# Edge messages of a graph layer: the last three groups are left out of the table until its squares have been summed, and the barrier between the two stages goes

## What is computed

```python
h = jnp.maximum(_layernorm(x, axis=-1), 0.0)
z = jnp.concatenate([h[src], h[dst], edge_attr_32], axis=-1)
m = jax.nn.sigmoid(z @ W_f + b_f) * jax.nn.softplus(z @ W_s + b_s)      # one row for each edge
message = jax.ops.segment_sum(m, src, num_segments=100000)
mean = jnp.mean(message, axis=0)
var = jnp.mean((message - mean) ** 2, axis=0)
out = x + h + (message - mean) * jax.lax.rsqrt(var + 1e-5) * gamma + beta
```

## Time and profile before

| | us |
|---|---|
| median of 3 runs | 1090.13 (1090.04 to 1090.58) |
| profiled execution | 1098.08 |
| its span, first to last instruction | 1096.2 |
| POOL busy in the span | 691.6 (63%) |
| DVE busy | 730.7 (67%) |
| ACT busy / PE busy | 541.5 (49%) / 561.5 (51%) |
| first block load of the scan issued | 900.60 |
| last block of the scan landed | 964.70 |

### The profile page before, as it was taken

How to read it: one execution, slowest core, us unless ns; L and a number is a source line. 1 busy time by engine, 2 the same in 40 slices (tenths; PEclk the granted TensorE clock), 3 DMA queues, 4 the chain that set the end, 5 groups by cost and what they waited for, 6 DMA issues and landing times. The chain is left out here.

```text
span 1096.2 us, 10749 instructions
## 1 busy us (share of the span) xinstructions
PE 561.5 (51%) x2286; PEld 386.8 (35%) x2286; DVE 730.7 (67%) x1514; ACT 541.5 (49%) x1201; POOL 691.6 (63%) x606
## 2 busy tenths in 40 slices
PE   1131745566554476374575455765545636744423
PEld 0120533445442354252353234553333425630000
DVE  3211765758766667666686756767657676789978
ACT  1122655456555566464565454755554634644432
POOL 7774777777777787877877778777777540010000
PEclk9985676566576756656766765655666658975555
DMA  8992435345434354334344333334243339979999
GB/s 288 407 388 52 95 82 124 80 115 123 102 93 107 88 121 124 78 61 83 54 85 84 58 82 74 62 87 85 53 85 57 54 59 397 420 273 420 427 427 396
DMA packets 85856, 174.00 MB, mean 159 GB/s; under 512 B 40591, under 2 KB 47411, under 8 KB 77491
## 3 DMA queue, kind: packets, MB, share of 16 engines
q1 hardware_dynamic: 34523, 109.88, 28.4%
q0 software_dynamic: 40768, 19.31, 15.4%
q10 hardware_dynamic: 10520, 44.39, 10.1%
HBM read 105.67 MB, written 67.85 MB: 158 GB/s over the span
## 5 line engine op out<-in xcount | busy, mean ns | idle before, releaser
L411 POOL DMA_INDIRECT xg<-in_x_dram,ids x392 | 375.6, 958 | 120.9 <-issue 116.1
L424 POOL DMA_INDIRECT msgs_dram<-comb,target x196 | 309.6, 1580 | 87.7 <-issue 71.2
L843 PE MATMUL bank_c<-msg,same 128*128 128x64 f32 x980 | 165.8, 343 | 32.8 <-issue 19.7
L843 PEld LDWEIGHTS bank_c<-msg,same 128*128 128x128 f32 x980 | 158.0, 254 | 46.4 <-issue 25.2
L516 DVE TENSOR_REDUCE row_ssq<-sq 128x24 f32<-128x1536 f32 (+2 forms) x53 | 86.5, 1631 | 113.5 <-ACT sq L699 58.9
L811 PE MATMUL bank_c<-ident,eas 128*128 128x128 f32 x49 | 21.2, 432 | 248.8 <-ACT comb L754 247.9
L754 ACT ACTIVATE comb<-bank_c 128x256 f32<-128x256 f32 x49 | 18.6, 380 | 212.0 <-remote 208.2
L832 PEld LDWEIGHTS ps_v<-w_z,z_t 128*128 128x128 f32 x392 | 93.2, 326 | 49.8 <-issue 49.8
L747 ACT ACTIVATE same<-same,one_col 128x512 f32<-128x512 f32 x196 | 107.6, 550 | 1.6
L599 DVE TENSOR_TENSOR msg<-gate,soft 128x256 f32<-128x256 f32 x49 | 20.7, 423 | 126.7 <-issue 71.8
L811 PEld LDWEIGHTS bank_c<-ident,eas 128*128 128x128 f32 x49 | 8.8, 180 | 262.9 <-issue 262.8
(11 more groups left out here) (120 smaller groups left out, 989.0 us busy)
## 6 DMA issues: line engine op xcount, KB each, us to landing
m_buf<-msgs_dram SPq DMA_DIRECT2D x37, 1024.0 KB, 20.6
xn<-in_x_dram SPq DMA_DIRECT2D x48, 512.0 KB
out_dram<-m_buf ACTq DMA_DIRECT2D x20, 1024.0 KB, 10.5
msgs_dram<-y_kept SPq DMA_DIRECT2D x11, 1536.0 KB
src_all<-src_rows_dram SPq DMA_DIRECT2D x46, 256.0 KB
y_spill_dram<-y_kept ACTq DMA_DIRECT2D x19, 512.0 KB
y_kept<-y_spill_dram SPq DMA_DIRECT2D x8, 1024.0 KB, 20.6
msgs_dram<-y_kept ACTq DMA_DIRECT2D x5, 1536.0 KB
```

The source lines that it names most:

```text
L411: pool.indirect_dma_start(xg[:, n % G_SLOTS, 2 * j + c, :], None, x, bass.IndirectOffsetOnAxis(ap=ids[:, c, n * TILES + j:n * TILES + j + ...
L424: pool.indirect_dma_start(msgs, bass.IndirectOffsetOnAxis(ap=target[:, n % UNROLL, j:j + 1], axis=0), comb[:, n % UNROLL, j, :], None, com ...
L843: pe.matmul(ps_c[:, j, :], same[:, b, j, :], msg[:, b, :], start=(b == 0), stop=(b == j))
```

## The change

Stages one and two become one program per engine without a barrier; stage one's buffers now lie in `m_buf`, `m_last` and `sums`, so that the first five blocks of the ring (`FREE_FIRST`) and the others come free at different points. The nodes no longer trail (`SKEW` 0). The messages of groups 46 to 48 (`LATE` = 3) stay on chip (`late_comb`, `late_msg`). POOL gathers the table's rows for their 12 tiles (`was_read`), scatters them into a second table `msgs_late`, gathers them back from there (`added_late`), and DVE works out by how much the squares grow, `late_msg * (2 * was_read + added_late)`, and sums it into `corr_row` (`correct`, after block 15's squares). When the scan's loads have landed, the 12 tiles are added to `msgs` (`add_late`), and after the held blocks are stored, scaled and added to `out` (`patch`). `msgs_late` is filled with zeros, one piece of 512 KB in each step from group 6 on and the rest at group 48. The ring has 8 blocks in place of 9, the edge-attribute ring 3 slots in place of 6, `comb` 3 in place of 6.

```diff
-SKEW = 4
+SKEW = 0
...
-E_SLOTS = 6
+E_SLOTS = 3
+COMB_SLOTS = 3
+LATE = 3
+EARLY = GROUPS - LATE
...
-M_BUFS = 9
+M_BUFS = 8
+FREE_FIRST = 5
...
-Y_AHEAD = 3
+Y_AHEAD = 6
+CORRECT_AT = 15
+LIST_AT = 10
...
+            if not g.known:
+                sp.dma_start(late_rows[:, bass.ds((g.n - UNROLL) * BULK, BULK), :].rearrange("p r f -> p (r f)"),
+                             zeros[:, :]).then_inc(late_zeroed, 16)
...
-            for n in range(behind, GROUPS):
+        for n in range(behind, EARLY):
                 accumulate(n)
-            pool.wait_ge(accumulated, 16 * ALL_TILES)
+        pool.wait_ge(late_listed, 1)
+        pool.wait_ge(ssq_done, STEPS)
+        pool.wait_ge(accumulated, 16 * TILES * EARLY)
+        for k in range(LATE):
+            n = EARLY + k
+            for t in range(k * TILES, (k + 1) * TILES):
+                pool.indirect_dma_start(
+                    was_read[:, t, :], None, msgs, bass.IndirectOffsetOnAxis(ap=late_ids[:, t:t + 1], axis=0),
+                ).then_inc(late_read, 16)
+            pool.wait_ge(comb_copied, n + 1)
+            pool.wait_ge(target_done, n + 1)
+            if k:
+                pool.wait_ge(late_put, 16 * TILES * k)
+            else:
+                pool.wait_ge(late_zeroed, 16 * (LAST - UNROLL + 3))
+            for j in range(TILES):
+                pool.indirect_dma_start(
+                    msgs_late, bass.IndirectOffsetOnAxis(ap=target[:, n % UNROLL, j:j + 1], axis=0),
+                    late_comb[:, k * TILES + j, :], None, compute_op=ALU.add,
+                ).then_inc(late_put, 16)
+        pool.wait_ge(late_put, 16 * LATE_TILES)
+        for t in range(LATE_TILES):
+            pool.indirect_dma_start(
+                added_late[:, t, :], None, msgs_late, bass.IndirectOffsetOnAxis(ap=late_ids[:, t:t + 1], axis=0),
+            ).then_inc(late_got, 16)
...
-            act.wait_ge(spilled, 16 * SPILL)
...
+    def sync(sp):
+        sp.wait_ge(accumulated, 16 * TILES * EARLY)
+        sp.wait_ge(y_done, STEPS)
+        sp.wait_ge(z_turned, GROUPS)
+        sp.wait_ge(ea_turned, GROUPS)
...
+            if b == FREE_FIRST:
+                sp.wait_ge(sum_kept, 1)
+                sp.wait_ge(comb_copied, GROUPS)
+                sp.dma_start(m_rest[:, :], msgs[P * N_ROWS:NODES, :]).then_inc(rest_loaded, 16)
+            if b == NB - 1:
+                sp.wait_ge(corr_done, 1)
...
+        sp.wait_ge(late_added, 16 * LATE_TILES)
+        sp.wait_ge(block_crossed, M_BUFS + 2)
...
+                if k == len(y_parts) - 1:
+                    act.wait_ge(patched, 16 * LATE_TILES)
...
+        def correct():
+
+            dve.wait_ge(late_read, 16 * LATE_TILES)
+            dve.wait_ge(late_got, 16 * LATE_TILES)
+            dve.scalar_tensor_tensor(out=was_read, in0=was_read, scalar=2.0, in1=added_late,
+                                     op0=ALU.mult, op1=ALU.add).then_inc(corr_steps, 1)
...
+            if i == len(held) - 1 and y_parts[k + 1][0] > i:
+                dve.wait_ge(late_added, 16 * LATE_TILES)
...
```

More of the change, by code:

```diff
@@ L60 @@
 assert 0 < LAST_ROWS < BULK
-assert (SPILL + 1 + SKEW) % UNROLL == 0
+assert (SPILL + 1 + SKEW) // UNROLL >= 1 and UNROLL % COMB_SLOTS == 0 and LATE <= UNROLL
 S_BLK = 32
@@ L116, in first_row, with late @@
     @property
+    def late(self):
+        return self.known and self.n >= EARLY
+    @property
     def first_row(self):
@@ L158, in keep @@
             return outer.enter_context(nc.sbuf_tensor(name, shape, dt))
[L160 to L168, removed]
@@ new lines, in build @@
+        at = Shared()
+        at.y_kept = keep("y_kept", [P, KEPT_ROWS, F])
+        at.ones = keep("ones", [P, P])
+        at.ident = keep("ident", [P, P])
+        at.eps_col = keep("eps_col", [P, 1])
+        at.one_col = keep("one_col", [P, 1])
+        at.msg_sum = keep("msg_sum", [P, F])
+        at.small = keep("small", [P, 4])
+        at.target = keep("target", [P, UNROLL, TILES], I32)
+        at.late_comb = keep("late_comb", [P, LATE_TILES, F])
+        at.late_msg = keep("late_msg", [P, LATE_TILES, F])
@@ L377, in _ @@
-            for u in range(SLOTS):
-                load(Group(0, u))
-            sp.wait_ge(zeros_set, 1)
-            done = ZERO_EARLY
-            for u in range(SLOTS, UNROLL + 1):
-                end = min(ZERO_PARTS, 2 * ZERO_EARLY + 1 + 3 * (u - SLOTS))
-                for k in range(done, end):
-                    zero_table(k)
-                done = end
-                if u < UNROLL:
-                    load(Group(0, u))
-            with sp.Fori(1, ITERS) as it:
-                for u in range(UNROLL):
-                    load(Group(it, u))
@@ L391, in _ @@
-            for u in range(GROUPS - LAST + SKEW):
-                load(Group(ITERS, u))
+            one.sync(sp)
+            two.sync(sp)
         @block.gpsimd
         def _(pool):
-            pool.sem_inc(slots_free, UNROLL - 1)
-            pool.memset(ident[:, :], 0.0).then_inc(masks_set, 1)
-            pool.memset(upto[:, :], 1.0).then_inc(masks_set, 1)
-            pool.wait_ge(masks_set, 2)
-            pool.affine_select(out=ident[:, :], in_=ident[:, :], compare_op=ALU.not_equal, fill=1.0,
-                               base=0, pattern=[[-1, P]], channel_multiplier=1).then_inc(masks_made, 1)
@@ L444, in _ @@
[L444 to L446 removed]
+            one.gpsimd(pool)
+            two.gpsimd(pool)
         @block.vector
         def _(dve):
[L450 to L455 removed]
@@ L649, in _ @@
-            for u in range(1, UNROLL):
-                step(Group(0, u), True)
-            first_kept = (SPILL + 1 + SKEW) // UNROLL
-            with dve.Fori(1, first_kept) as it:
-                for u in range(UNROLL):
-                    step(Group(it, u), True)
-            with dve.Fori(first_kept, ITERS) as it:
-                for u in range(UNROLL):
-                    step(Group(it, u), False)
-            for u in range(STEPS - LAST + 1):
-                step(Group(ITERS, u), False)
@@ L780, in _ @@
-            for u in range(UNROLL):
-                step(Group(0, u), True)
-            first_kept = (SPILL + 1 + SKEW) // UNROLL
-            with act.Fori(1, first_kept) as it:
-                for u in range(UNROLL):
-                    step(Group(it, u), True)
-            with act.Fori(first_kept, ITERS) as it:
-                for u in range(UNROLL):
-                    step(Group(it, u), False)
-            for u in range(STEPS - LAST + 1):
-                step(Group(ITERS, u), False)
```

1980 lines of the change are left out of this document (1103 added, 877 removed).

## The result

The changed kernel takes 1099.46 us (median of four runs, 1098.57 to 1101.91), the kernel before 1090.32 beside it (1090.04 to 1090.58). The ratio is 1.009, with a 95% interval of 1.0078 to 1.0103: the change costs 9 us. The prediction had 1083.6 and a faster kernel at 0.62, a slower one at 0.28. The time lies inside its range, on the wrong side. The profiled execution took 1099.36, with a span of 1097.6.

What follows compares the result with a forecast made beforehand. POOL's indirect DMAs were taken to bound stage one, the DMA engines the scan and output part. -17.5 (scan) + 7 (output part) + 4 (start) = -6.5 from 1090.1 gave 1083.6 us, range 1070 to 1102.

Steps and rivals of the forecast that it cites:

- Steps 1 and 2: End of stage one: five early scan loads leave at 864.5, 36.1 us earlier; the sixth load's wait opens at 888.
- Steps 2 and 3: Scan from 888: ramp 3.3, remaining blocks 49.6, POOL's 36 indirect DMAs 6.3 us; last block lands 947.2, 17.5 us gained.
- Step 4: Scan: POOL's correction data arrive at 921 to 928, DVE finishes at 939 to 946, just before the last block; cost 0.
- The rule of the Trainium skill: Scan: DMA engines take turns between queues packet by packet, so landings stay in the single figures of us.
- Step 5: Output part, after the scan's last block lands: one more block reloaded, late reloads and patches together cost +7 us.
- The ring's 2.5: Output part: the ring holds 8 blocks, so one more is reloaded, 1.05 MB at 427 GB/s, +2.5 us.
- their lateness: Output part: reloads wait for the late scatters, until 38 us after the scan's last block lands; cost +1 us.
- The patches: Output part: 12 scatters into `out` at 0.29 us each, +3.5 us, ending far from the end.
- Step 6: Start of stage one: extra loads and spills ahead of the last zero writes; cost 0 or +9, middle +4 us taken.
- the first of its two cases: Start: POOL's wait for ACT's first copy is apart from the write burst; cost 0, or below 0 if it moves forward.
- Step 7: Stage one's steady part: 25.6 MB more of zeros and three `comb` slots cost 0.
- Of the rivals the first: Scan and output part: correction and late scatters come too late, landings over 6 us; 1090 to 1122 us, chance 0.19.

Runs made afterwards that it cites:

- g3: The kernel before with its ring of blocks cut from 9 buffers to 8; 1092.94 us, ratio 1.0026 to the kernel before.
- the second trace of before: The kernel before unaltered, profiled again later, with its last `comb` copy 8 us earlier than in the recorded trace; 1090.14 us in one execution.
- g2: The changed kernel without the correction (`corr_row` set to zero) and without the second table's 25.6 MB of zeros; 1076.98 us, ratio 0.9884 to the kernel before.

## Why the prediction was wrong, and where it was right

*Steps 1 and 2, the early loads and the gate.* Right in kind. The first loads left at 861.41 (864.5 forecast). The gate opened at 875.67 and not at 888: 8 us of that are the level, since the prediction read a trace of the upper one and the result was measured on the lower, and 4 are a real gain over the forecast.

*Steps 2 and 3, the bytes.* Right. From the gate to the last of the other blocks the forecast had 57 us (3.3 + 47.3 + 6.3); the windows show the loads running from 876 to about 932, at 383 to 409 GB/s in place of 421.

*Step 4, is the correction in time: the step that failed.* It put the cost at 0, and two of its terms were wrong. The chain was forecast to deliver at 921 to 928 and delivered at 933.3: the 37.5 us and the 15 us of instructions were right, but the landings were 5.6 us beyond what four gathers hide, and 9.54, where it had 0 and 2.5 to 5.8. The larger error was the slack. DVE was to finish at 939 to 946, ahead of the last block at 947.2, so that a wait of up to 8 us was free and only "from 928 on each microsecond of lateness shows". That slack came from 1.8 us a block, which is DVE's adds alone and leaves out the hand-over with ACT; a block took 2.1. From the gate to block 15 DVE needed 38.8 us (914.82 - 876.03; 3.8 until its first add) where the step had 32, and behind the correction 19.2 (956.16 - 936.95; four subtractions of the mean are among them) where it had 14.4. Gate to shift without a stall is 63.6 and 3.6 for the correction, 67.2, which is just what the prediction had for the loads (947.2 + 8.0 - 888). So nothing was left to hide in, and the whole stall of 18.5 us counted from its first microsecond: 85.7, measured 85.9. DVE reached block 15 at 914.8, not at 920, because the gate was early; what made the loads earlier made the wait longer. `shift` was forecast 17.5 us ahead of before and came 2.7 ahead: 14.8 lost. From the gate (67.2 forecast, 85.9 measured) it is 18.7, less the 4 of the earlier gate.

*The rule of the Trainium skill* that the prediction weighed ("DMA: Bandwidth & Descriptors", Queues, rings and completion order) is about turns between queues and gives no size; the single figures were the prediction's own estimate from it. The trace agrees with the rule so far that a landing during the scan stayed well below the loads' own 20.6 us: 10.7 and 9.54, against 2.42 behind stage one. The estimate was too low there, and by more in the output part (12.61 and 17.10, see below).

*Step 5, the output part, +7 forecast, 12.1 measured.* The ring's 2.5 was right (2.4 in g3). The reloads came later than forecast (`shift` + 30 forecast, + 38 measured), and their lateness was priced at 1, measured 5.3, of which 3.2 are the queue of `y` that was seen in the code and given no price. The patches were 3.5 forecast, 5.1 measured.

*Step 6, the start, +4 forecast.* It cost nothing. POOL's first scatter is at 105.98 (106.59 before, rows 8), after a wait of 12.35 us in place of 13.02 (the second trace of before, on the same level as the result, has 105.86 and 12.25); the first of its two cases.

*Step 7, the steady part.* Right: the copies keep ahead, g2 bounds the zeros at 2 us.

*The sum.* -6.5 + 14.8 + 5.1 - 4 = 9.4, and the spans differ by 1097.6 - 1088.2 = 9.4. Of the rivals the first is what happened, with landings of the 10 us that it names. It priced them at 1094 because it, too, let DVE's stall hide up to the last block.

**What stays open.** Why stage one's last messages come at two levels 8 us apart is not settled. In the new trace of before the copies already run some 18 us ahead around 300 us while POOL's pace is the same; no row names what lets them. That the patches slow the other traffic is shown; by what means is not, and the rate accounts for 2.5 of their 5 us.

## What to carry to other kernels

An instruction that waits for another engine's chain, put at a fixed place into the stream of an engine with no slack, turns all its lateness into time. Put it as late as its result allows; here five blocks later was worth 13 us. When loads are moved forward, first add up the time of the engines that consume them, with their waits for each other and not only their busy time, since that sum, and no longer the DMA engines, may set the end. And what is to land beside the loads lands later when they come earlier. Two waits that hold the same queue hide each other: each taken away alone looks free.

## What the runs showed of the hardware

The landing of four accumulating scatters, from the end of the last one to the next instruction that waits for it, is 2.42 us behind stage one, 10.7 and 9.54 during the scan, and in the output part 12.61 and as in these rows of the changed kernel's POOL:

```profile
983.42 2.13 POOL L1364 DMA_INDIRECT msgs_dram<-late_comb,target  x1 [6.92 <-DMA msgs_dram<-late_comb,target]
...
1059.90 1.54 POOL L1374 DMA_INDIRECT out_dram<-late_comb,late_out  x1 [17.10 <-DMA out_dram<-late_comb,late_out]
```

I had not expected them to grow to 17 us. Nor that twelve scatters of 128 rows of 256 bytes, 0.4 MB in all, would take the whole rate from 427 to 412 GB/s over 70 us and cost 5 us, where their share of the engines in the earlier trace rows gave 3.5.
